# A routed feed-forward stage: table copies and gathers in another order on GpSimd, the first expert tile's transpose behind the third gathered tile, constants last

## Chip, cores and metric
One core of a Trainium2 chip. The metric is the device time of one launch in microseconds, the median of several runs. The program runs once from start to end; nothing is repeated inside it.

## What is computed
A pre-norm block on 2048 tokens of width 512, in float32: linear attention with 32 heads of 64, then a mixture of 8 experts (two chosen per token, hidden width 352). The part that matters here is the second half:

```python
scores = xf @ gate_w.T + gate_b + bias
top_scores, top_idx = jax.lax.top_k(scores, TOP_K)          # TOP_K = 2, E = 8
gates = jax.nn.softmax(top_scores, axis=-1)
comb = jnp.sum(one_hot(top_idx, E) * gates[..., None], axis=1)
h = jax.nn.silu(jnp.einsum('td,ehd->teh', xf, w1) + b1)
y = jnp.einsum('teh,edh->ted', h, w2) + b2
out = x + jnp.einsum('ted,te->td', y, comb)
```

## The kernel before, in words
Every product is made of three matmuls: each operand is split into a rounded part ("hi", on ScalarE, ACT) and the rest ("lo", on VectorE, DVE). Each engine has its own instruction list, written out by hand; semaphores join them, and an instruction behind a wait on the same engine waits too. Direct loads are issued by SyncE (SP), gathers and scatters by GpSimd (POOL).

The first 780 us are attention and the routing of each of 16 token tiles: GpSimd scatters token number and gate into a table in DRAM (`meta_dram`, line 676). What follows is the stretch around the change.

**Weights.** The expert weights go through 46 steps, k = 0 to 45: steps 0 to 21 are w1 (`W1T` is 22), steps 22 to 45 are w2, three for each expert (expert 6 is k = 40 to 42, expert 7 is k = 43 to 45). In step k TensorE transposes 128 columns' worth of the loaded weights into PSUM (`w_transpose`, line 1899, matmuls at line 1895), ACT copies the hi part (`w_hi`, line 1102, line 1105), and DVE subtracts to get the lo part (`w_lo`, line 1532, line 1536). For the steps in `PE_STEPS` TensorE subtracts instead (`subtract_hi`, line 1919) and ACT copies (line 1110). There are six PSUM banks, so step k waits for the lo part of step k - 6. The first step of an expert also waits for its load (`s_w2[e]`) and for `b2_put`, GpSimd's small copies of the bias into column 352 of the loaded weights (`put_b2`, line 722). SP loads w2 of experts 6 and 7 (`load_w2`, line 526) only once `s_metain` says that the slot table has come back (line 562).

**Slot table.** GpSimd works out which table row each slot has (lines 755 to 761), waits for all scatters (`s_meta`) and gathers the table to SBUF (`meta_in`, line 764). Then it works out the expert of each of the 39 slot tiles (`cmp`, lines 767 to 769; `padt`, `tile_expert`, lines 772 and 773). TensorE transposes the table behind step 35 (`meta_transpose`, line 1952, with `meta_put`), and DVE turns it into `slot_token` (line 1563, `ids_ready`) and `far` (line 1564); where DVE does so in its list of weight steps is the constant `META_AT`.

**Expert tiles.** A tile i is 128 slots of one expert (NS = 39 tiles). GpSimd gathers its rows (`gather`, line 694) into one of two buffers `xg`; gather(i) waits until tile i - 2 has been transposed. TensorE transposes it (`pe_gT`, line 1965, line 1970), ACT and DVE split it (`act_gT` line 1131, `dve_gT` line 1577; the lo parts carry the helper's line 1212), TensorE multiplies with w1 (`pe_h`, line 1973), ACT copies h out of PSUM (`act_h`, line 1137), TensorE transposes h (`pe_hT`, line 1982), ACT applies silu with the bias (`act_silu`, line 1143), DVE splits it (`dve_hT`, line 1581), TensorE multiplies with w2 (`pe_y`, line 1991), DVE scales by the gate (`dve_y`, line 1589), and GpSimd adds the rows to the output with an accumulating scatter (`add_out`, line 702). `hT_fill` (line 1567) writes h's constant rows (a one for the bias, zeros) once. From tile 2 on the order is a loop; tiles 0 to 2 are started by hand:

```python
            pe_gT(0, 0)                      # line 2006; w_transpose(44), w_transpose(45) behind it
            pe_gT(1, 1)                      # line 2012
            pe_h(0, first_expert)            # line 2015
            pe_h(1, expert(1))
            pe_hT(0)
            pe_gT(2, 0)
            pe_hT(1)                         # line 2020, then the loop with pe_h(2)
```

Of the kernel before, what the change touches and what calls it, by code (L numbers as in the profile page):

```python
# [30 lines left out]
ALU = mybir.AluOpType  # L31
# [16 lines left out]
E = 8  # L48
# [6 lines left out]
TW = NS + 1  # L55
# [8 lines left out]
def block_kernel(nc, x, Wq, Wk, Wv, Wo, bo, gate_w, gate_b, gbias, w1, b1, w2, b2, out):  # L64
# [110 lines left out]
    def small_sb(name, cols, dt=F32):  # L175
        at_ = used[0]
        used[0] += -(-(2 if dt is BF16 else 4) * cols // 32) * 32
        assert used[0] <= R2 + 4 * KB
        return sb(name, cols, at_, dt)

    iota_e = small_sb("iota_e", E)
    iota_j = small_sb("iota_j", TW)
# [16 lines left out]
    cmp = small_sb("cmp", TW * E)  # L199
# [26 lines left out]
    with ExitStack() as ctx:  # L226
# [3 lines left out]
        def sem(name):  # L230
            return ctx.enter_context(nc.semaphore(name))
# [96 lines left out]
        w_put = sem("w_put")  # L328
# [3 lines left out]
        w_sub_put = sem("w_sub_put")  # L332
# [40 lines left out]
        PE_STEPS = [*range(4), 11, 15, 19, 22, 25, 31, 37]  # L373
# [20 lines left out]
        wide = lambda a, n: a.unsqueeze(2).to_broadcast([P, a.shape[1], n])  # L394
        many = lambda a, n: a.unsqueeze(1).to_broadcast([P, n, a.shape[1]])
        by8 = lambda a: a.rearrange("p (n e) -> p n e", e=E)
        tiles_of, up_to, spare, past = (small[:, i * E:(i + 1) * E] for i in range(4))
# [174 lines left out]
        def _(pool):  # L572
# [121 lines left out]
            def gather(i):  # L694
                if i == 0:
                    pool.wait_ge(ids_ready, 1)
                if i >= 2:
                    pool.wait_ge(gT_put, i - 1)
                pool.indirect_dma_start(xg[:, i % 2 * D:(i % 2 + 1) * D], None, xn2_dram,
                                        bass.IndirectOffsetOnAxis(slot_token[:, i:i + 1].bitcast(U32), 0)).then_inc(s_g[i % 2], 16)  # L700
# [21 lines left out]
            def put_b2(e):  # L722
                pool.tensor_copy(w2_in[e][:, :].rearrange("p (f n) -> p f n", f=FB)[:, :, H:H + 1],
                                 b2T[:, e * FB:(e + 1) * FB].unsqueeze(2)).then_inc(b2_put, 1)
# [9 lines left out]
            def tab(ins):  # L734
                tabled[0] += 1
                ins.then_inc(table_step, 1)
                pool.wait_ge(table_step, tabled[0])

            def fold(a, n):
                while n > 1:  # L740
                    n //= 2
                    tab(pool.tensor_tensor(a[:, :, 0:n], a[:, :, 0:n], a[:, :, n:2 * n], ALU.add))
# [16 lines left out]
            fold(row8, E)  # L759
            tab(pool.tensor_tensor(row8[:, :, 0:1], row8[:, :, 0:1], iota_p[:, :].unsqueeze(1), ALU.add))  # L760
            tab(pool.tensor_scalar(meta_row[:, :].unsqueeze(1), row8[:, :, 0:1], float(MROWS - 1), None, ALU.min))
            for b in range(2):
                pool.wait_ge(s_meta[b], 16 * NT)
            pool.indirect_dma_start(meta_in[:, :], None, meta_rows, bass.IndirectOffsetOnAxis(meta_row[:, :].bitcast(U32), 0)
                                    ).then_inc(s_metain, 16)

            tab(pool.tensor_tensor(by8(cmp[:, :]), wide(iota_j[:, :], E), many(up_to, TW), ALU.subtract))
            tab(pool.tensor_scalar(by8(cmp[:, :]), by8(cmp[:, :]), 0.0, None, ALU.is_ge))
            fold(by8(cmp[:, :]), E)
            pool.wait_ge(w_put, W1T)  # L770
            pool.wait_ge(w_sub_put, W1_SUBS)
            tab(pool.tensor_copy(padt[:, :].unsqueeze(2), by8(cmp[:, :])[:, :, 0:1]))
            pool.tensor_scalar(tile_expert[:, :], padt[:, :], float(E - 1), None, ALU.min).then_inc(experts_ready, 1)
            put_b2(6)
            put_b2(7)
            gather(0)
            gather(1)
            gather(2)
            pool.wait_ge(experts_ready, 1)
            tab(pool.iota(add_iota[:, :], pattern=[[16, TW // 2], [0, 2]], base=16, channel_multiplier=0))  # L780
# [26 lines left out]
        def _(act):  # L807
# [323 lines left out]
            def act_gT(i):  # L1131
                act.wait_ge(gT_put, i + 1)
                if not (isinstance(i, int) and i < 2):
                    act.wait_ge(h_put, i)
                nc.scalar.copy(g_of(i)[0][:, :], g_bank(i)).then_inc(gT_hi_ready, 1)

            def act_h(i):
                act.wait_ge(h_put, i + 1)
                if not (isinstance(i, int) and i == 0):
                    act.wait_ge(hT_put, i)  # L1140
                nc.scalar.copy(h_in[:, :], h_bank(i)).then_inc(h_ready, 1)

            def act_silu(i, e):
                act.wait_ge(hT_put, i + 1)
                if not (isinstance(i, int) and i == 0):
                    act.wait_ge(hT_lo_ready, i)
                for b in range(HB):
                    w = min(P, H - b * P)
                    last = nc.scalar.activation(hT[0:w, b * P:(b + 1) * P], hT_bank(i)[0:w, b * P:(b + 1) * P], ACT.Silu,  # L1149
                                                bias=b1T[0:w, ds(b * E + e, 1)])  # L1150
                last.then_inc(hT_ready, 1)
# [15 lines left out]
            nc.scalar.activation(gate_e[:, :], far[:, :], ACT.Tanh, scale=0.5).then_inc(tanh_ready, 1)  # L1167
            act.wait_ge(experts_ready, 1)
            first_expert = act.value_load(tile_expert[0:1, 0:1], min_val=0, max_val=E - 1)
            act.wait_ge(hT_ones, 2)  # L1170
            act_h(0)
            act_h(1)
            act_gT(2)
            act_silu(0, first_expert)
            act_silu(1, act.value_load(tile_expert[0:1, 1:2], min_val=0, max_val=E - 1))
            with act.Fori(2, NS - 1) as i:
# [5 lines left out]
        def _(dve):  # L1182
# [28 lines left out]
            def lo(dst, src, hi):  # L1211
                return nc.vector.tensor_tensor(dst, src, f(hi), ALU.subtract)  # L1212
# [319 lines left out]
            def w_lo(k):  # L1532
                dve.wait_ge(w_hi_ready, k + 1)
                src, rows, dst = w_step(k, w1_lo, w2_lo, w_bank(k))
                hi = w_step(k, w1_hi, w2_hi, w_bank(k))[2]
                nc.vector.tensor_tensor(dst, src, f(hi), ALU.subtract).then_inc(w_lo_ready, 1)

            v = nc.vector
            META_AT = 32
            lo_steps = lambda a, b: [w_lo(k) for k in range(a, b) if k in DVE_STEPS]  # L1540

            def tiles_per_expert():
# [15 lines left out]
            lo_steps(6, 11)  # L1558
            put_slot8(NT - 1, 1)
            tiles_per_expert()  # L1560
            lo_steps(11, META_AT)
            dve.wait_ge(meta_put, 1)
            v.tensor_copy(slot_token[:, :], pX[:, 0:TW]).then_inc(ids_ready, 1)
            v.tensor_copy(far[:, :], pX[:, TW:2 * TW]).then_inc(far_ready, 1)
            lo_steps(META_AT, WSTEPS - 2)

            def hT_fill():
                dve.wait_ge(w_put, WSTEPS)
                v.memset(hT[96:128, 2 * P:3 * P], 0.0).then_inc(hT_ones, 1)
                dve.wait_ge(hT_ones, 1)  # L1570
                v.memset(hT[96:97, 2 * P:3 * P], 1.0).then_inc(hT_ones, 1)

            def put_gates():
                dve.wait_ge(tanh_ready, 1)
                v.tensor_scalar(slot_gate[:, :], gate_e[:, :], -0.5, 0.5, ALU.mult, ALU.add).then_inc(gates_ready, 1)

            def dve_gT(i):
                dve.wait_ge(gT_hi_ready, i + 1)
                lo(g_of(i)[1][:, :], g_bank(i), g_of(i)[0][:, :]).then_inc(gT_lo_ready, 1)
# [16 lines left out]
            dve_gT(0)  # L1596
            for k in range(WSTEPS - 2, WSTEPS):
                w_lo(k)
            hT_fill()
            dve_gT(1)  # L1600
            put_gates()
            dve_gT(2)
            dve_hT(0, 0)
# [21 lines left out]
        def _(pe):  # L1625
# [339 lines left out]
            def pe_gT(i, b):  # L1965
                pe.wait_ge(s_g[b], 16 * (i // 2) + 16 if isinstance(i, int) else 8 * i + (16 - 8 * b))
                if not (isinstance(i, int) and i < 2):
                    pe.wait_ge(gT_lo_ready, i)
                for n in range(FB):
                    last = nc.tensor.transpose(g_bank(i)[:, n * P:(n + 1) * P], xg[:, b * D + n * P:b * D + (n + 1) * P], ident[:, :])  # L1970
                last.then_inc(gT_put, 1)

            def pe_h(i, e):
                pe.wait_ge(gT_lo_ready, i + 1)
                if not (isinstance(i, int) and i < 2):
                    pe.wait_ge(h_ready, i)
                for n in range(FB):
                    last = three(h_bank(i), two(g_of(i), n * P, P), two((w1_hi, w1_lo), e * H + n * EH, H),
                                 n == 0, n == FB - 1)
                last.then_inc(h_put, 1)  # L1980

            def pe_hT(i):
                pe.wait_ge(h_ready, i + 1)
                if not (isinstance(i, int) and i < 2):
                    pe.wait_ge(hT_ready, i)
                for n in range(HB):
                    w = min(P, H - n * P)
                    last = nc.tensor.transpose(hT_bank(i)[0:w, n * P:(n + 1) * P], h_in[:, n * P:n * P + w], ident[:, :])  # L1988
                last.then_inc(hT_put, 1)
# [13 lines left out]
            def expert(i):  # L2003
                return pe.value_load(tile_expert[0:1, ds(i, 1)], min_val=0, max_val=E - 1)
# [9 lines left out]
            pe.wait_ge(w_act_ready, len(PE_STEPS))  # L2014
            pe_h(0, first_expert)
            pe_h(1, expert(1))
            pe_hT(0)
            pe_gT(2, 0)
            pe.wait_ge(w_lo_ready, len(DVE_STEPS))
            pe_hT(1)  # L2020
            with pe.Fori(1, NS // 2) as h:
# [35 lines left out]
```

## Time and profile before

| what | us |
|---|---|
| median of 3 runs | 1009.13 |
| lowest and highest | 1009.12, 1009.3 |
| the profiled execution's own time | 1010.6 |
| its span, first to last instruction | 1008.9 |
| TensorE busy in the span | 995.8 (99%) |
| DVE, ACT, GpSimd busy | 688.1, 513.2, 255.7 |

The granted TensorE clock is 1.0 throughout. The profiled execution took 1.5 us more than the median; its rows are from its span. Times in rows are from the span's start. A group "x8" of matmuls on one line is two weight steps or two tiles of four. The idle time in brackets is that of the engine just before the row, with what ended it; where a wait has several semaphores, the profile names the one that it takes for the last.

### The profile page before, as it was taken

What the parts mean: (1) busy time and instruction counts of PE and PEld (TensorE: products, weight loads), DVE (VectorE), ACT (ScalarE), POOL (GpSimd) and SP (SyncE); (2) the same over time, 40 slices, a digit from 0 to 9 for tenths busy, and PEclk for the clock granted to TensorE, in tenths of its full rate; (3) what the DMA queues carried; (4) which work ended last, traced back from release to release, by engine and by line L of the source; (5) the groups of instructions that cost most, each with busy time, mean ns of one, the idle gap of its engine ahead of it and who ended that gap; (6) DMA issues with size and microseconds to landing.
All of it is one profiled execution on the core that took longest, in us unless ns stands there. A gap on an engine that the chain in (4) does not pass through costs nothing.

```text
span 1008.9 us, 17463 instructions
## 1 busy us (share of the span) xinstructions
PE 995.8 (99%) x5019; PEld 839.2 (83%) x5020; DVE 688.1 (68%) x1554; ACT 513.2 (51%) x1322; POOL 255.7 (25%) x413
## 2 busy tenths in 40 slices
PE   8999999999999999999999999999999989999998
PEld 7888888888888888888788888888888879989996
DVE  6888655665666677767878778887888764544544
ACT  5444444444444447755556555555554954343442
POOL 1000000000000002222433232333333555555554
PEclk9999999999999999999999999999999999999999
DMA  7002501000000012343211121111125645555653
GB/s 263 13 30 84 209 22 40 23 21 21 21 22 21 21 63 63 105 172 116 44 44 51 42 52 42 42 42 42 42 66 149 203 123 102 107 102 101 107 108 48
DMA packets 46862, 75.35 MB, mean 75 GB/s; under 512 B 6090, under 2 KB 18555, under 8 KB 46691
## 3 DMA queue, kind: packets, MB, share of 16 engines
q1 hardware_dynamic: 37010, 56.04, 18.3%
q0 software_dynamic: 9808, 18.79, 10.2%
q8 instruction: 21, 0.34, 0.1%
q14 instruction: 23, 0.18, 0.1%
HBM read 53.14 MB, written 23.50 MB: 76 GB/s over the span
## 4 chain that ended last, share of the span: by engine, by line
PE 93%; DVE 3%; ACT 1%; DMA 1%; issue 1%; SPq 0%; POOL 0%; POOLq 0%; DVEq 0%; ACTq 0%
PE pK L1627 16%; PE pK L1629 16%; PE pK L1628 16%; PE pA L1627 6%; PE pA L1629 6%; PE pA L1628 6%; PE pX L1627 6%; PE pX L1629 5%; PE pX L1628 5%; PE pA L1761 3%; PE pT L1970 2%; PE pT L1707 2%; PE pX L1988 1%; PE pA L1895 1%; PE pK L1895 1%; DMA xn<-in_attn_hidden_states 1%
## 5 line engine op out<-in xcount | busy, mean ns | idle before, releaser
L973 ACT ACTIVATE qs<-q,nrec 128x64 f32<-128x64 f32 x512 | 129.6, 336 | 88.1 <-DVE nrec L1357 85.7
L594 POOL TENSOR_TENSOR wv_lo<-wv_in,wv_hi 128x512 fp32r<-128x512 f32 x4 | 5.2, 1296 | 403.5 <-ACT wo_hi L894 403.5
L1627 PE MATMUL pA<-k_hi,xn_hi 128*128 128x512 f32 x256 | 100.9, 394 | 0.6 <-DVE k_lo L1232 0.6
L1627 PE MATMUL pK<-wk_hi,xnT_hi 128*128 128x512 f32 (+1 forms) x256 | 100.1, 391 | 0.4 <-DVE wk_lo L1212 0.3
L1627 PE MATMUL pK<-wq_hi,xnT_hi 128*128 128x512 f32 x256 | 100.4, 392 | 0.0
L1629 PE MATMUL pK<-wq_hi,xnT_lo 128*128 128x512 f32 x256 | 99.9, 390 | 0.0
L1629 PE MATMUL pA<-k_hi,xn_lo 128*128 128x512 f32 x256 | 99.8, 390 | 0.0
L1628 PE MATMUL pK<-wk_lo,xnT_hi 128*128 128x512 f32 (+1 forms) x256 | 99.7, 390 | 0.0
L1628 PE MATMUL pA<-k_lo,xn_hi 128*128 128x512 f32 x256 | 99.7, 389 | 0.0
L1629 PE MATMUL pK<-wk_hi,xnT_lo 128*128 128x512 f32 (+1 forms) x256 | 99.7, 389 | 0.0
L1628 PE MATMUL pK<-wq_lo,xnT_hi 128*128 128x512 f32 x256 | 99.7, 389 | 0.0
L1627 PE MATMUL pX<-m_hi,qsT_hi 128*128 128x512 f32 x240 | 99.1, 413 | 0.0
L1629 PE MATMUL pX<-m_hi,qsT_lo 128*128 128x512 f32 x240 | 94.2, 393 | 0.0
L1628 PE MATMUL pX<-m_lo,qsT_hi 128*128 128x512 f32 x240 | 93.7, 390 | 0.0
L1350 DVE TENSOR_TENSOR qs<-q,ksum 128x512 f32<-128x512 f32 x64 | 51.8, 810 | 55.6 <-ACT q L967 55.6
L718 POOL DMA_INDIRECT out<-y,slot_token x38 | 66.1, 1739 | 68.8 <-DVE y L1593 43.3
L1232 DVE SCALAR_TENSOR_TENSOR k_lo<-pK,k_hi 128x512 fp32r<-128x512 f32 x64 | 44.1, 689 | 56.1 <-ACT k_hi L841 56.1
L835 ACT CAST xn_hi<-xn 128x512 fp32r<-128x512 f32 x64 | 39.8, 621 | 69.3 <-PE pA L1629 69.3
L967 ACT ACTIVATE q<-pK 128x512 f32<-128x512 f32 x64 | 38.2, 597 | 68.3 <-PE pK L1629 68.3
L841 ACT ACTIVATE k_hi<-pK 128x512 fp32r<-128x512 f32 x64 | 38.0, 595 | 66.4 <-PE pK L1629 66.3
L1149 ACT ACTIVATE hT<-pX,b1T 128x128 f32<-128x128 f32 (+1 forms) x114 | 33.2, 363 | 71.5 <-PE pX L1988 63.8
L1212 DVE TENSOR_TENSOR xn_lo<-xn,xn_hi 128x512 fp32r<-128x512 f32 x64 | 44.1, 689 | 27.6 <-ACT xn_hi L835 27.6
(291 smaller groups left out, 2446.8 us busy)
## 6 DMA issues: line engine op xcount, KB each, us to landing
w_in<-in_ffn_w SPq DMA_DIRECT2D x22, 256.0 KB, 4.2
w_in<-in_ffn_w SPq DMA_DIRECT2D x8, 704.0 KB, 5.8
xn<-in_attn_hidden_states SPq DMA_DIRECT2D x16, 256.0 KB, 6.2
wv_in<-in_attn_Wv SPq DMA_DIRECT2D x16, 256.0 KB, 2.8
wo_in<-in_attn_Wo SPq DMA_DIRECT2D x16, 256.0 KB, 3.0
wk_in<-in_attn_Wq SPq DMA_DIRECT2D x4, 1024.0 KB, 5.7
xnT_dram<-xnT SPq DMA_DIRECT2D x4, 1024.0 KB, 11.5
x_in<-in_attn_hidden_states SPq DMA_DIRECT2D x16, 256.0 KB, 2.7
```

Source lines behind the costliest of these rows:

```text
L718: pool.indirect_dma_start(out, bass.IndirectOffsetOnAxis(slot_token[:, i:i + 1].bitcast(U32), 0), rows, None, bounds_check=T - 1, oob_is_e ...
L835: nc.scalar.copy(xn_hi[:, b * D:(b + 1) * D], xn[:, ds(t * D, D)]).then_inc(xn_hi_ready, 1)
L841: nc.scalar.activation(k_hi[:, b * CW:(b + 1) * CW], pK[:, b * 512:(b + 1) * 512], ACT.Relu).then_inc(k_hi_ready, 1)
L967: nc.scalar.activation(q[:, b * CW:(b + 1) * CW], pK[:, b * 512:(b + 1) * 512], ACT.Relu).then_inc(q_ready, 1)
L973: i = nc.scalar.activation(qs[:, s], q[:, s], ACT.Copy, scale=nrec[:, b * HC + h:b * HC + h + 1])
L1149: last = nc.scalar.activation(hT[0:w, b * P:(b + 1) * P], hT_bank(i)[0:w, b * P:(b + 1) * P], ACT.Silu, bias=b1T[0:w, ds(b * E + e, 1)])
L1212: return nc.vector.tensor_tensor(dst, src, f(hi), ALU.subtract)
L1232: nc.vector.scalar_tensor_tensor(out=k_lo[:, s], in0=pK[:, b * 512:(b + 1) * 512], scalar=0.0, in1=f(k_hi[:, s]), op0=ALU.max, op1=ALU.sub ...
L1350: nc.vector.tensor_tensor(qs[:, b * CW:(b + 1) * CW], q[:, b * CW:(b + 1) * CW], ksum[:, c * CW:(c + 1) * CW], ALU.mult).then_inc(qk_ready, 1)
L1627: nc.tensor.matmul(dst, lhs[0], rhs[0], start=start, stop=False)
L1628: nc.tensor.matmul(dst, lhs[0], rhs[1], start=False, stop=False)
L1629: return nc.tensor.matmul(dst, lhs[1], rhs[0], start=False, stop=stop)
```

## The change
Four places.

1. GpSimd: the first two instructions on `cmp` move ahead of the wait for the scatters and of the table's gather.
2. GpSimd: gather(0) and gather(1) move ahead of the bias copies of experts 6 and 7.
3. DVE: weight steps 32 and 33 move ahead of the two copies out of the transposed table. Since the wait for `meta_put` no longer stands ahead of them, they get waits of their own, for step 33's transpose and for the subtraction of step 31. `hT_fill` moves behind the lo part of tile 1.
4. TensorE: the transpose of tile 2 goes ahead of that of tile 0's h. ACT: tile 2's hi part goes ahead of the copy of tile 1's h, and the wait for the constants moves down to the first silu.

```diff
@@ GpSimd
             tab(pool.tensor_scalar(meta_row[:, :].unsqueeze(1), row8[:, :, 0:1], float(MROWS - 1), None, ALU.min))
+            tab(pool.tensor_tensor(by8(cmp[:, :]), wide(iota_j[:, :], E), many(up_to, TW), ALU.subtract))
+            tab(pool.tensor_scalar(by8(cmp[:, :]), by8(cmp[:, :]), 0.0, None, ALU.is_ge))
             for b in range(2):
                 pool.wait_ge(s_meta[b], 16 * NT)
             pool.indirect_dma_start(meta_in[:, :], None, meta_rows, bass.IndirectOffsetOnAxis(meta_row[:, :].bitcast(U32), 0)
                                     ).then_inc(s_metain, 16)
 
-            tab(pool.tensor_tensor(by8(cmp[:, :]), wide(iota_j[:, :], E), many(up_to, TW), ALU.subtract))
-            tab(pool.tensor_scalar(by8(cmp[:, :]), by8(cmp[:, :]), 0.0, None, ALU.is_ge))
             fold(by8(cmp[:, :]), E)
...
             pool.tensor_scalar(tile_expert[:, :], padt[:, :], float(E - 1), None, ALU.min).then_inc(experts_ready, 1)
+            gather(0)
+            gather(1)
             put_b2(6)
             put_b2(7)
-            gather(0)
-            gather(1)
             gather(2)
@@ ACT
             first_expert = act.value_load(tile_expert[0:1, 0:1], min_val=0, max_val=E - 1)
+            act_h(0)
+            act_gT(2)
+            act_h(1)
             act.wait_ge(hT_ones, 2)
-            act_h(0)
-            act_h(1)
-            act_gT(2)
             act_silu(0, first_expert)
@@ DVE
-            META_AT = 32
+            META_AT = 34
...
-            lo_steps(11, META_AT)
+            lo_steps(11, 32)
+            dve.wait_ge(w_put, 34)
+            dve.wait_ge(w_sub_put, sum(k < 32 for k in PE_STEPS))
+            lo_steps(32, META_AT)
             dve.wait_ge(meta_put, 1)
             v.tensor_copy(slot_token[:, :], pX[:, 0:TW]).then_inc(ids_ready, 1)
...
                 w_lo(k)
+            dve_gT(1)
             hT_fill()
-            dve_gT(1)
             put_gates()
@@ TensorE
             pe_h(0, first_expert)
             pe_h(1, expert(1))
+            pe_gT(2, 0)
             pe_hT(0)
-            pe_gT(2, 0)
             pe.wait_ge(w_lo_ready, len(DVE_STEPS))
             pe_hT(1)
```

## Rows read from the trace of the kernel before

**Rows 1.** Busy time by stretch: start:end, length, engines busy (instructions), clock, DMA share, GB/s

```profile
806.80:816.03 9.23, 7.56 (x57) 6.12 (x56) 8.01 (x15) 7.44 (x15) 4.82 (x12) 1.00 0.62 213
816.03:822.89 6.86, 5.66 (x35) 4.90 (x35) 2.92 (x8) 2.82 (x8) 4.92 (x15) 1.00 0.28 80
827.68:999.20 171.52, 171.52 (x1006) 154.87 (x1004) 84.32 (x144) 67.81 (x179) 96.01 (x69) 1.00 0.56 99
```

**Rows 2.** The chain that ended last, from 811 to 816: start, length, what

```profile
811.17 1.06 PE pA L1895 x8
...
813.12 0.64 PE pK L1895 x4
...
815.09 0.70 DVE gT_lo L1212
```

**Rows 3.** Tile w_in, SP's issues from 805 to 816 (experts 6 and 7)

```profile
L527 SPq DMA_DIRECT2D w_in<-in_ffn_w x2: 367/434/501, 806.8 to 807.2; - x2
...
DMA to landing us min/median/max: 5.8/5.8/5.8
```

**Rows 4.** DMA queues from 808 to 812: packets, MB, share of 16 engines

```profile
q1 hardware_dynamic: 958, 1.33, 98.4%
```

**Rows 5.** DMA queues from 812.5 to 814

```profile
q0 software_dynamic: 136, 0.43, 76.4%
```

**Rows 6.** Timeline of GpSimd from 803 to 817: start, length, what

```profile
803.20 1.12 POOL L764 DMA_INDIRECT meta_in<-meta_dram,meta_row  x1 [2.04 <-DMA meta_dram<-vals,slot_i]
804.34 0.75 POOL L767 TENSOR_TENSOR cmp<-iota_j,small 128x320 f32<-128x320 f32 x1
805.18 1.04 POOL L768 TENSOR_SCALAR cmp<-cmp 128x320 f32<-128x320 f32 x1
...
808.83 1.06 POOL L699 DMA_INDIRECT xg<-xn_dram,slot_token  x1
810.20 0.95 POOL L699 DMA_INDIRECT xg<-xn_dram,slot_token  x1 [0.31 <-issue]
...
816.65 1.00 POOL L699 DMA_INDIRECT xg<-xn_dram,slot_token  x1 [0.50 <-POOL add_base L781]
```

**Rows 7.** Timeline of DVE from 807 to 818

```profile
807.39 0.20 DVE L1563 CAST slot_token<-pX 128x40 int32<-128x40 f32 x1 [1.75 <-PE pX L1956]
...
807.61 2.48 DVE L1536 TENSOR_TENSOR w_lo<-pA,w_hi 128x512 fp32r<-128x512 f32 x4
...
817.06 0.17 DVE L1569 MEMSET hT<- 32x128 f32 x1
...
817.50 0.69 DVE L1212 TENSOR_TENSOR g_lo<-pA,g_hi 128x512 fp32r<-128x512 f32 x1
```

**Rows 8.** Timeline of TensorE from 805 to 822

```profile
805.64 0.47 PE L1923 MATMUL pK<-w_hi,neg_ident 128*128 128x512 f32 x1
...
818.34 0.42 PE L1627 MATMUL pA<-w_hi,g_hi 128*128 x1
...
820.37 0.49 PE L1988 MATMUL pX<-ident,h_in 128*128 128x128 f32 x3
820.69 0.60 PE L1970 MATMUL pT<-ident,xg 128*128 128x128 f32 x4
821.55 0.52 PE L1988 MATMUL pA<-ident,h_in 128*128 128x128 f32 x3 [0.25 <-ACT h_in L1141]
822.89 0.42 PE L1627 MATMUL pK<-w_hi,gT_hi 128*128 x1 [0.82 <-DVE gT_lo L1212]
```

**Rows 9.** Timeline of ACT from 820 to 823

```profile
820.95 0.45 ACT L1141 COPY h_in<-pA 128x352 f32<-128x352 f32 x1 [2.19 <-PE pX L1988]
821.33 0.59 ACT L1135 CAST gT_hi<-pT 128x512 fp32r<-128x512 f32 x1
```

**Rows 10.** DMA queues from 799 to 801

```profile
q1 hardware_dynamic: 330, 0.44, 60.4%
q0 software_dynamic: 60, 0.00, 2.1%
```

## Prediction
> **What bounds the kernel now.** I read three views in turn. The busy time by stretch comes first: TensorE is busy for all of 171.52 us from 827.68 on, while it stands idle for 1.67 us of 806.80 to 816.03 and 1.20 us of 816.03 to 822.89 [rows 1]. The expert loop is full, so a change ahead of it is worth what it moves the loop's first matmul, tile 2's pe_h at 822.89 [rows 8]; that shift then rides to the end unchanged, for the closing scatters follow TensorE.
>
> The chain that ended last comes second, for the nearer limits. Ahead of tile 0's product it runs through step 43 (TensorE at 813.12, ACT, DVE), then tile 0's lo part at 815.09, ending 815.79; pe_h(0) starts at 816.03 (0.24 later) [rows 2]. Why does step 43 start only at 813.12? It is expert 7's first step. SP issued the loads of experts 6 and 7 at 806.8 and 807.2, and they land 5.8 us after issue, so at about 813.0 [rows 3]. Step 40 at 811.17 is expert 6's first step, and I read it as held by its load too: the lo part of step 34, which it also needs, is the third of the four from 807.61 on, done by about 809.5 [rows 7]. Meanwhile the 16 DMA engines are full (98.4%) and all of it is SP's queue, q1 [rows 4]; GpSimd's queue q0, with gathers issued at 808.83 and 810.20 [rows 6], moves its rows after 812.5, as q1 has run dry [rows 5].
>
> So the stretch before 816 hangs on one release: SP may load experts 6 and 7 once the slot table's gather has landed. That gather was issued at 803.20 [rows 6] and SP went on at 806.80, 3.6 us later.
>
> The timelines come third, for who is free when.
>
> **Part 1, cmp ahead of the table's gather.** Removed behind the gather: 0.75 + 1.04 us of GpSimd. Added ahead of it: the same two. GpSimd was idle for 2.04 us before 803.20, so from 801.16 [rows 6]. With the 0.09 us between these two (805.09 to 805.18) they run 801.25 to 802.00 and 802.09 to 803.13. That looks like a fit under 803.20. But the gather now follows a chained operation whose semaphore it must wait for, and gather(3), which does just that, starts 0.50 us after the operation ahead of it [rows 6]. That gives 803.63, which is **0.43 us late**. Bounds: 0 if the copies run faster or the start cost overlaps; 0.5 if they run a little slower beside DVE. I take 0.43, since the row for it is the same kind of instruction behind the same kind of wait. Behind this gather are queued: SP's two loads (+0.43, to 807.23), and TensorE's table transposes, behind which steps 36 to 39 wait. The latter is covered: TensorE then waits for expert 6's load anyway. The loads landing 0.43 later are not covered: step 43 moves to 813.55, pe_h(0) to 816.46. What GpSimd gains (the expert numbers over 1 us earlier) is worth nothing, since ids_ready holds gather(0) and TensorE reads the expert number only behind step 45.
>
> **Part 2, gathers ahead of the bias copies.** ids_ready comes at about 808.0 (the slot_token copy ended at 807.59 [rows 7] and the table lands 0.43 later), so gather(0) starts 0.14 to 0.50 us later, about 808.3 instead of 808.83, and gather(1) 1.37 us behind it, at 809.7. By [rows 4, 5] their rows move after q1 has drained whatever the issue time, so they gain nothing: cost 0. The bias copies, which ended just ahead of 808.83, now follow gather(1) and end at about 811.1; who waits is step 40, free from about 811.5 (its load). Cover 0.4 us; if the gathers' issue took longer, step 40 and then DVE's chain would slip by the excess. gather(2) still waits for tile 0's transpose, so its issue moves by the same 0.43; tile 2's transpose, now earlier, still comes about 5 us behind it.
>
> **Part 3, DVE.** DVE was free from 805.64 (1.75 us before 807.39) [rows 7]. The new waits are met at 806.11, when the subtraction of step 31 ends [rows 8]; queued behind them are steps 32 and 33 and the two copies. Steps 32 and 33 take 0.62 each (2.48 for four) [rows 7] and end near 807.5; the table, 0.43 later, lets the copies start at 807.82. Without the 0.43 the copies would be some 0.1 us late. DVE comes to step 34 over half a microsecond earlier, and step 40 doesn't gain from it while its load is last. Cost 0, gain 0. The memsets leave the front of tile 1's lo part: 817.06 to 817.50, so 0.44 us earlier, ending 817.75 instead of 818.19 [rows 7]. pe_h(1) ran from 818.34 to 820.37, 2.03 us; pe_h(0) has the same twelve matmuls from 816.03, so could hand over at 818.06. The lo part's old end, 818.19, was 0.13 past that, and the start another 0.15 behind it [rows 8]. Gain 0.13 to 0.28; I take **0.2**, the middle. The constants themselves are needed by the first silu, which ACT does behind 821.33 [rows 9], and are written at about 818.2: hidden with over 3 us.
>
> **Part 4, tile 2 ahead of h.** On TensorE the three transposes of h(0) cost 0.32 (820.37 to 820.69) [rows 8] ahead of tile 2's. On ACT the copy of h(1) stood ahead of tile 2's hi part, 0.38 from start to start [rows 9]; both ended in a tie at 821.33. With both gone tile 2's hi part starts 0.3 earlier, with the 0.2 of part 3 about 0.5 earlier, at 820.85 (in the old trace's time). DVE has nothing else then, and pe_h(2) follows the lo part as before, at 822.41. Next in line is h(1): ACT's copy comes after the hi part, at 821.35 to 821.45, and ends 0.45 later; hT(1) started 0.15 behind it (821.40, 821.55), so at 821.95 to 822.05, and with 0.33 for three transposes it is over by 822.3 to 822.4. That is nearly a tie, so I take **0.45** for the memsets' and the order's gain together. Silu of tile 0 stands behind the same two ACT instructions as before, so at the same time; its user, pe_y(0), stands behind pe_h(2), 2 us long, and doesn't come to wait.
>
> **Sum.** +0.43 - 0.45 = -0.02 us on the profiled execution: 1010.6 stays 1010.6. The median lies 1.5 us lower, 1009.13, and I carry the same difference over: 1009.1.
>
> **The rivals.** Case A, the above: +0.43 (0.3 to 0.5) and -0.45 (-0.5 to -0.3), so 1009.0 to 1009.3.
>
> Case B: the table's gather isn't late. If the 0.50 us start cost was already inside the 2.04 us idle (scatters landed at 802.7 and the gather took its time), or the two copies are quicker in an idle stretch, then 803.2 stays. For it: the idle is put down to a DMA, whose landing isn't shown. Then only -0.45 is left: 1008.7, with the bounds 1008.5 to 1008.8.
>
> Case C, slower: gathers 0 and 1 are issued half a microsecond sooner and SP's loads 0.43 later, so gather rows get in before expert 7's weights. The engines moved 1.33 MB from 808 to 812 with the first packets only after 808.3 [rows 4], so nearly 0.4 MB/us; a gather of 128 rows of 2 KB is 0.26 MB, so one ahead costs 0.66 us, both 1.33. Against: no packet of q0 from 808 to 812 although gather(0) had been issued by 809.9 [rows 4, 6]. For: earlier, small scatters of q0 do have 60 packets beside 330 of q1 within 2 us [rows 10]. It decides once gather(0)'s descriptors stand ready before SP's last ones. Net 0.43 + 0.66 - 0.45 = +0.6, or +1.3 with both: 1009.8 to 1010.4. The Trainium skill (DMA: Bandwidth & Descriptors, section Queues, rings and completion order) says that each DMA engine takes turns between the queues that have work, packet by packet; by that rule the two queues would share, and earlier gathers would push the loads back, up to this case. The rows show no sharing where gather(0) waited, so I give it a low chance.
>
> Case D: part 4's gain is lost in the near tie (hT(1) late, since it now waits for an ACT copy that comes 0.4 later), or the bias copies pass 811.5. Then +0.43 - 0.45 + 0.2 to 0.4: 1009.3 to 1009.5.
>
> **How the numbers follow.** A 0.45, B 0.25, C 0.15, D 0.15. The likeliest is A, so 1009.1. For 8 in 10 the range takes all of A, D and B, and the lower half of C: 1008.4 to 1010.0, with 0.1 to spare below B's lowest. What a measurement of this kernel can tell from no change is about 0.2%, here 2.0 us. No case reaches that: B is -0.6 at most and C +1.3. I leave 0.02 for faster and 0.03 for slower by something that I don't see; same 0.95.
>
> **What would show it.** In the changed profile: cmp's two instructions end near 803.1, and the table's gather starts at 803.6 (A) or 803.2 (B). SP's loads start 3.6 us behind it. Step 43 at 813.5 (A), 813.1 (B), or over 814 (C); in C there would be q0 packets between 809 and 812. From pe_h(0) to pe_h(2) 6.86 us become about 6.4; if hT(1) ends last there, it is D. Wrong would be: a loop that is no longer full, or pe_h(2) more than 0.7 us off 822.9.

## The result, and the profile after

The changed kernel takes 1011.69 us (median of 14 runs, 1010.01 to 1012.88) against 1009.4 (14 runs, 1008.7 to 1010.78): +2.3 us, a ratio of 1.002 with a 95% interval of 1.0013 to 1.0027. Forecast were 1009.1 and a range up to 1010.0. The changed kernel is **slower**, by an amount that is small (0.2%; by a bound of 2% the two are the same) but clear of its interval, and that no case of the prediction reached. Three executions of the kernel before among those beside the later kernels took 1422 to 4806 us; they are left out of every ratio and count.

The profiled execution shows almost none of that. It took 1010.63 us with a span of 1008.9, the kernel before 1010.6 and 1008.9. Both are single executions; before's lies near the upper end of its 14 runs, after's near the lower end. So two traces side by side look the same, and the medians don't. Below, h(1) is tile 1's h as ACT copies it out of PSUM, and hT(1) is its transpose on TensorE (`pe_hT`). The busy time by stretch, after, in the stretches of [rows 1]:

```profile
806.80:816.03 9.23, 7.45 (x58) 6.34 (x57) 7.67 (x15) 7.42 (x15) 3.76 (x7) 1.00 0.62 213
816.03:822.89 6.86, 5.21 (x35) 4.72 (x34) 3.06 (x9) 2.69 (x8) 4.98 (x14) 1.00 0.27 78
827.68:999.20 171.52, 171.52 (x1006) 154.88 (x1004) 84.37 (x143) 67.81 (x179) 95.99 (x69) 1.00 0.56 99
```

The loop is as full as before. TensorE is idle for 1.65 us of the second stretch, where it was 1.20. Its timeline there, after (what answers to [rows 8]):

```profile
810.95 1.06 PE L1898 MATMUL pA<-ident,w_in 128*128 128x128 f32 x8 [0.97 <-DMA w_in<-in_ffn_w]
...
812.91 0.63 PE L1898 MATMUL pK<-ident,w_in 128*128 128x128 f32 x4 [0.46 <-issue]
...
815.83 0.43 PE L1630 MATMUL pK<-w_hi,gT_hi 128*128 x1 [0.34 <-DVE gT_lo L1212]
...
817.85 0.32 PE L1630 MATMUL pA<-w_hi,g_hi 128*128 x1
...
819.77 0.60 PE L1973 MATMUL pT<-ident,xg 128*128 128x128 f32 x4
820.21 0.49 PE L1991 MATMUL pX<-ident,h_in 128*128 128x128 f32 x3
821.68 0.52 PE L1991 MATMUL pA<-ident,h_in 128*128 128x128 f32 x3 [0.98 <-ACT h_in L1141]
822.87 0.42 PE L1630 MATMUL pK<-w_hi,gT_hi 128*128 x1 [0.67 <-issue]
```

pe_h(1) at 817.85 follows pe_h(0) at once, as planned, and is 0.49 ahead of its old time. But pe_h(0) itself, at 815.83, is 0.20 ahead of its old time, where the forecast had it 0.43 behind. The table's gather is only 0.12 late in this trace (GpSimd's timeline, after):

```profile
802.00 1.03 POOL L763 TENSOR_SCALAR cmp<-cmp 128x320 f32<-128x320 f32 x1
803.32 1.12 POOL L766 DMA_INDIRECT meta_in<-meta_dram,meta_row  x1 [0.29 <-POOL cmp L763]
```

SP went on 3.43 us behind it instead of 3.60, and step 43 came 6.16 us behind SP's issue instead of 6.32. Then hT(1) waits 0.98 us for the copy of h(1), and pe_h(2) a further 0.67 for "issue", that is for nothing that another engine does. Tile 2's lo part had long been there, by DVE's timeline (with ACT's two rows ahead of it):

```profile
820.41 0.59 ACT L1135 CAST gT_hi<-pT 128x512 fp32r<-128x512 f32 x1 [1.91 <-PE pT L1973]
821.09 0.45 ACT L1141 COPY h_in<-pA 128x352 f32<-128x352 f32 x1
```

```profile
821.03 0.69 DVE L1212 TENSOR_TENSOR gT_lo<-pT,gT_hi 128x512 fp32r<-128x512 f32 x1 [2.94 <-ACT gT_hi L1135]
```

It ended at 821.72, and pe_h(2) started 1.15 us later. What stands between hT(1) and pe_h(2) is the fetch of tile 2's expert number by TensorE's own sequencer, at the head of the loop. The view of that line's instructions, after:

```profile
L2007 PEldq TENSOR_LOAD <-tile_expert x2: 311/312/312, 816.7 to 821.9; - x2
L2007 PEldq FUSED_REGOPS  x2: 151/154/156, 817.1 to 822.3; - x2
L2007 PEldq SEQ_ASSERT  x2: 18/18/18, 817.3 to 822.5; - x2
```

The load starts at 821.9, behind hT(1), and what belongs to it ends past 822.5. The kernel before fetched at 821.9 too, which its view shows in the same way, with DVE's row for the lo part behind it:

```profile
L2004 PEldq TENSOR_LOAD <-tile_expert x1: 311/311/311, 821.9 to 821.9; - x1
```

```profile
821.95 0.69 DVE L1212 TENSOR_TENSOR gT_lo<-pT,gT_hi 128x512 fp32r<-128x512 f32 x1 [3.66 <-ACT gT_hi L1135]
```

So in the kernel before the lo part (over at 822.64) and the fetch (over past 822.5) met at nearly the same time, and the profile named only the first of them [rows 8].

### The profile page after: what moved, and what is told of

It is laid out like the page before. It is cut to its first block, busy times and chain, and to the rows that moved or that the text cites. A ratio compares the mean times of both kernels' runs of the same rounds, so it can differ in the third digit from the quotient of the medians.

```text
span 1008.9 us, 17464 instructions
## 1 busy us (share of the span) xinstructions
PE 995.6 (99%) x5019; PEld 839.2 (83%) x5020; DVE 690.0 (68%) x1554; ACT 513.3 (51%) x1322; POOL 255.2 (25%) x413
## 4 chain that ended last, share of the span: by engine, by line
PE 93%; DVE 3%; DMA 2%; ACT 1%; issue 1%; POOL 0%; SPq 0%; POOLq 0%; DVEq 0%; ACTq 0%
PE pK L1630 16%; PE pK L1632 16%; PE pK L1631 16%; PE pA L1630 6%; PE pA L1632 6%; PE pA L1631 6%; PE pX L1630 5%; PE pX L1632 5%; PE pX L1631 5%; PE pA L1764 3%; PE pT L1973 2%; PE pT L1710 2%; PE pX L1991 1%; PE pA L1898 1%; PE pK L1898 1%
## 5 line engine op out<-in xcount | busy, mean ns | idle before, releaser
L1350 DVE TENSOR_TENSOR qs<-q,ksum 128x512 f32<-128x512 f32 x64 | 55.1, 861 | 53.9 <-ACT q L967 53.9
```

The lines of the kernel that those rows point to most:

```text
L1350: nc.vector.tensor_tensor(qs[:, b * CW:(b + 1) * CW], q[:, b * CW:(b + 1) * CW], ksum[:, c * CW:(c + 1) * CW], ALU.mult).then_inc(qk_ready, 1)
```

## The experiments

The theories differ in where the 2.3 us lie: in part 4 (S), in GpSimd's parts (G), or nowhere in particular (L). The four first kernels split the change.

**e1_order4: part 4 alone.**

```diff
-            act.wait_ge(hT_ones, 2)
             act_h(0)
-            act_h(1)
             act_gT(2)
+            act_h(1)
+            act.wait_ge(hT_ones, 2)
...
-            pe_hT(0)
             pe_gT(2, 0)
+            pe_hT(0)
```

> The kernel before with part 4 alone: TensorE transposes tile 2 ahead of tile 0's h, ACT does tile 2's hi part ahead of h(1), and waits for the constants at the first silu. Theory S (the loss is local: the new order gathers TensorE's idle time into fewer, longer pieces and something downstream then runs slower): this run alone shows the whole loss, +2.3 us on 1009.4, and the rest of the change none. Theory G (the loss comes from GpSimd's and the DMA queues' new order): 0 here, within 0.5 us. Theory L (the loss has no place in the changed stretch; it comes with any changed program, through how the instructions lie in memory or how the start falls): every variant is off by an amount of its own, between 0 and +3 us, and they do not add up. In the trace pe_h(2) starts at 822.9 as before, because the expert number for it is only fetched by TensorE's sequencer behind hT(1).

Measured: 1010.29 us, ratio 1.0011 (1.0002 to 1.002) to 1009.35. TensorE's timeline of this kernel:

```profile
814.94 0.42 PE L1627 MATMUL pK<-w_hi,gT_hi 128*128 x1 [0.34 <-DVE gT_lo L1212]
...
821.20 0.52 PE L1988 MATMUL pA<-ident,h_in 128*128 128x128 f32 x3 [0.98 <-ACT h_in L1141]
822.55 0.42 PE L1627 MATMUL pK<-w_hi,gT_hi 128*128 x1 [0.83 <-issue]
```

pe_h(0) to pe_h(2) takes 7.61 us instead of 6.86: part 4 is a loss of 0.75 us by itself. The eleven runs fall into two groups: eight at 1009.5 to 1010.6, three at 1011.4 to 1012.1, and these three have a mean granted clock of 0.997, the others 0.998 to 1.0.

**e2_no_order4: parts 1 to 3.** The changed kernel with the diff above undone, except that the wait for the constants stays at the silu.

> The changed kernel with part 4 undone (TensorE's and ACT's old order, the constants' wait just ahead of the first silu). Theory S: back to 1009.4 within 0.5. Theory G: 1011.7, the whole loss stays. Theory L: off by an amount of its own. In the trace pe_h(1) starts at once behind pe_h(0), hT(1) is no later than before, so pe_h(2) should be 0.2 to 0.5 us earlier than 822.9 if only the lo part and the sequencer's fetch hold it.

Measured: 1009.75 us, 1.0001 (0.9992 to 1.001); all runs at clock 0.998 or more. pe_h(0) to pe_h(2) is 6.38 us. So Theory S holds for most of the loss if part 4 is taken out of the change (1.9 us of the 2.3 go with it), but e1 with part 4 alone showed only 0.9. And step 43 came 7.04 us behind SP's issue, where it was 6.32. The DMA queues of this kernel from 812 to 812.5 show what goes with it:

```profile
q0 software_dynamic: 61, 0.19, 102.2%
q1 hardware_dynamic: 3, 0.00, 1.8%
```

Three last packets of SP's load (q1) go out in the midst of the gathers' rows (q0), 5.9 us or more behind SP's issue, and expert 7's load isn't complete before them.

**e3_gpsimd12: parts 1 and 2; e4_dve3: part 3.** Each is the kernel before with these lines of the diff alone; e4 (and h2 and i2 below) have ACT's wait for the constants at the first silu as well.

> The kernel before with parts 1 and 2 alone (cmp ahead of the table's gather, gathers 0 and 1 ahead of the bias copies). Theory G: the whole loss, +2.3 us. Theory S: 0 within 0.5. Theory L: an amount of its own. In the trace the table's gather starts at 803.3, as in the changed kernel.

> The kernel before with part 3 alone (weight steps 32 and 33 ahead of the table copies, constants behind tile 1's lo part; ACT's wait for them at the first silu). Theories S and G: 0 within 0.5, or 0.1 to 0.3 faster as pe_h(1) follows pe_h(0) at once. Theory L: an amount of its own.

Measured: e3 1010.04 us, 1.0006 (0.9997 to 1.0015); e4 1008.73, 0.9993 (0.9984 to 1.0002). The parts' shifts from 1009.35 are +0.9, +0.7 and -0.6; they add up to +1.0, and the change has +2.3. Each shift is uncertain by about 0.9 us, and e3's and e4's intervals reach no difference, so they count only together with the traces. Each shift has a matching piece there, which speaks against Theory L in its strong form, but 1.3 us are missing.

**f1_after_again: the changed kernel, unaltered.**

> The changed kernel once more, unaltered, for a second trace, since its 14 runs lie between 1010.0 and 1012.9 and the first trace (1010.63) is among the fastest. Eight of the 14 have a mean granted clock of 0.997. TensorE idles only at the end, for 4.9 us, which by the records explains down to 0.998. Theory K (clock): in those runs the clock is granted at its lower level for one stretch in the middle too, right behind the idle pieces between 820.7 and 822.9, and costs about 1.6 us there. Then a trace with 0.997 has such a stretch between 821 and 830, and its loop is late by 1.6 us. Theory T (tail): the extra time lies behind the last product, at the closing scatters, and the stretch up to there is as in the first trace.

(Counted again, seven of the fourteen have 0.997, not eight.) Measured: 1012.67 us, clock 0.997, and the trace has it. Busy time by stretch; the column ahead of the last two is the granted clock:

```profile
822.00:824.00 2.00, 1.13 (x5) 0.91 (x6) 1.16 (x3) 0.83 (x4) 1.10 (x1) 0.89 0.01 4
824.00:826.00 2.00, 2.00 (x8) 2.00 (x8) 0.92 (x2) 0.87 (x3) 0.00 (x0) 0.50 0.47 139
826.00:828.00 2.00, 2.00 (x11) 1.85 (x11) 0.00 (x0) 0.84 (x2) 0.16 (x1) 0.76 0.00 0
828.00:830.00 2.00, 2.00 (x13) 1.63 (x12) 1.00 (x2) 0.18 (x1) 0.78 (x1) 1.00 0.23 43
```

The clock stands at its lower level, 1.2 GHz instead of 2.4, through 824 to 826 and parts of the stretches on either side. Ahead of it TensorE had been idle for 0.98 and 0.67 us. What it costs is in the timeline of that run:

```profile
822.21 0.52 PE L1991 MATMUL pA<-ident,h_in 128*128 128x128 f32 x3 [0.98 <-ACT h_in L1141]
823.39 0.53 PE L1630 MATMUL pK<-w_hi,gT_hi 128*128 x1 [0.67 <-issue]
...
826.95 0.62 PE L1973 MATMUL pT<-ident,xg 128*128 128x128 f32 x4
```

The twelve matmuls of pe_h(2) take 3.56 us from 823.39 to 826.95, against 2.02 in the first trace: 1.54 us, and pe_h(2) to the last matmul grows by the same, from 180.74 to 182.27. Theory K holds; Theory T falls, since nothing is lost at the tail.

**f2_fill: the idle piece filled.**

```diff
             pe.wait_ge(w_lo_ready, len(DVE_STEPS))
+            keep_clock(8)
             pe_hT(1)
```

> The changed kernel with 8 idle transposes of the identity on TensorE between hT(0) and hT(1), into a PSUM bank that hT(1) overwrites. They lie in the 0.98 us in which TensorE waits for h(1), and should not delay hT(1) (8 x 0.11 us). Theory K: no run with clock 0.997 any more; median 1010.3 or a little below, 1.4 under the changed kernel's 1011.7. Theory T: 1011.7 as before, with half of the runs slow.

Measured: 1010.49 us, 1.001 (1.0001 to 1.0019) to 1009.5. hT(1) isn't held, and no run of eleven is at 0.997 (one is at 1012.1 with clock 1.0, so something else; what, isn't known). TensorE's timeline of this kernel, with the eight transposes (L1669):

```profile
820.71 1.04 PE L1669 MATMUL pA<-ident 128*128 128x128 f32 x8
821.76 0.55 PE L1991 MATMUL pA<-ident,h_in 128*128 128x128 f32 x3
822.94 0.42 PE L1630 MATMUL pK<-w_hi,gT_hi 128*128 x1 [0.62 <-issue]
```

The second idle piece, 0.62 us, is still there. Eight useless transposes take 1.2 us off the changed kernel.

**f3_idle: the kernel before with a later copy of h(1).**

```diff
             act_h(0)
+            act.wait_ge(h_put, 2)
+            act.wait_ge(hT_put, 1)
+            for n in range(6):
+                nc.scalar.activation(nrm[:, n:n + 1], eps[:, :], ACT.Silu)
             act_h(1)
```

> The kernel before with six one-column activations on ACT between the wait for hT(0) and the copy of h(1): the copy, hT(1), the fetch of the expert number and pe_h(2) all move back by the time that they take, 0.6 to 1.2 us, and TensorE is idle for that much more in one piece. Theory K: the delay itself, plus a share of runs that are slower by a further 1.6 us at clock 0.997, so a median of 1010.5 to 1012. Theory T: 1009.4 plus the delay and nothing else, no second group of runs.

Measured: 1010.76 us, 1.001 (1.0001 to 1.0019). The activations take 0.9 us, pe_h(2) is 7.50 behind pe_h(0). Six runs of twelve are at 0.997, with a median of 1011.6; the others' is 1010.1. This is the changed kernel's picture (idle pieces of 1.03 and 0.70 us around hT(1)), from the kernel before and one delay. Its profiled run is one of the six:

```profile
822.00:824.00 2.00, 1.76 (x7) 1.77 (x8) 1.01 (x3) 0.83 (x4) 0.04 (x1) 0.66 0.42 131
824.00:826.00 2.00, 2.00 (x9) 1.93 (x8) 0.92 (x2) 0.35 (x2) 0.00 (x0) 0.50 0.03 8
826.00:828.00 2.00, 2.00 (x12) 1.68 (x11) 0.69 (x1) 0.87 (x2) 0.94 (x1) 0.98 0.00 0
```

**f4_part1, g3_part1_late, g4_part2: GpSimd's parts apart.** f4 is the kernel before with part 1, g4 with part 2, and g3 is f4 and:

```diff
             put_b2(7)
+            pool.wait_ge(w_put, 39)
             gather(0)
```

> The kernel before with part 1 alone (cmp ahead of the table's gather). The four traces with and without it have the gather starting 6.0 us (with) and 5.2 to 5.8 us (without) behind the last scatter's issue. If that is the whole of the GpSimd parts' cost: +0.4 us, 1009.8, the same as parts 1 and 2 together. If the order of the gathers costs too (their rows ahead of expert 7's load, seen once in the second experiment's trace): +0.4 here against +0.7 for both.

> The kernel before with part 1, and a wait ahead of gather(0) for the transpose of step 38, so that the gather is issued some 2 us behind SP's loads as before and not 1.1 us. Theory Q (part 1 costs twice: the table's gather is 0.45 us late, and the early gather's rows get in ahead of the last packets of expert 7's weights, up to 0.7 us more): step 43 comes 6.2 to 6.3 us behind SP's issue, not 6.4 to 7.0, and the median is 1009.9, against 1010.4 for part 1 alone. If the second cost has nothing to do with when the gather is issued: 1010.4.

> The kernel before with part 2 alone: gathers 0 and 1 ahead of the bias copies. gather(0) is then issued 0.3 to 0.4 us earlier, some 1.6 us behind SP's loads. Theory Q: between nothing and +0.2 us, 1009.4 to 1009.6, as the gather still comes late. If the order of gathers and copies itself costs (step 40 waiting for the copies): step 40 starts later than 4.4 us behind SP's issue.

Measured: f4 1010.39 us, 1.0004 (0.9996 to 1.0013) to 1009.5; g3 1010.26, 1.0009 (1.0 to 1.0018) to 1009.43; g4 1009.68, 0.9999 (0.999 to 1.0008). By these medians part 1 carries the GpSimd parts' cost, though f4's interval reaches no difference. In g3 step 43 comes 6.32 us behind SP's issue, in f4 6.41: the late wait brings back only 0.1, in the trace as in the median. So as far as this tells the cost of part 1 alone is the table's later gather, and Theory Q's second half is worth little without parts 2 and 3. Step 40 in g4 starts 4.45 us behind SP's issue (before 4.37): the bias copies don't hold it.

**g1_hoist, g2_best, h3_best2, i1_best3: the fetch moved.** The fetch of tile 2's expert stands further ahead, and the loop's first pass is written out. g1 has this on the changed kernel, the others on parts 3 and 4 with GpSimd's order as before. In g1 and g2 it stands with tile 1's ahead of pe_h(1), in h3 both stand ahead of pe_h(0), in i1:

```diff
             pe_hT(0)
+            expert_2 = expert(2)
             pe.wait_ge(w_lo_ready, len(DVE_STEPS))
             pe_hT(1)
-            with pe.Fori(1, NS // 2) as h:
+            for i in (2, 3):
+                pe_h(i, expert_2 if i == 2 else expert(3))
+                pe_gT(i + 1, 1 - i % 2)
+                pe_y(i - 2, i % 2, expert(i - 2))
+                pe_hT(i)
+            with pe.Fori(2, NS // 2) as h:
```

> The changed kernel with the number of tile 2's expert fetched ahead of pe_h(1) instead of behind hT(1), and the loop's first pass (tiles 2 and 3) written out so that it can be used. Theory F (tile 2's product is held by the sequencer's fetch, 1.2 to 1.35 us behind hT(1), and not by its lo part): pe_h(2) follows hT(1) at once, 6.1 to 6.3 us behind pe_h(0) instead of 7.04, and the long idle piece is shorter, so hardly a run at clock 0.997; median 1009.4 to 1009.7. If instead the lo part of tile 2 holds it: 7.0 us and 1011.7 stay.

> Parts 3 and 4 with the fetch moved as in g1, but GpSimd's order as before. Theory F with the costs measured so far (GpSimd's parts +0.7, part 3 -0.4, part 4 with the fetch moved -0.3 instead of +0.7): 1008.5 to 1008.8, below the kernel before (1009.4) and no slower than part 3 alone (1008.7). Without Theory F: 1009.7.

> Parts 3 and 4, GpSimd's order as before, and the expert numbers of tiles 1 and 2 both fetched ahead of pe_h(0), where TensorE waits anyway (in g2 they stood between pe_h(0) and pe_h(1) and held the latter by 0.3 us). pe_h(1) 2.02 us and pe_h(2) 6.2 to 6.3 us behind pe_h(0); median 1008.5, 0.9 under the kernel before and 0.2 under part 3 alone; no run at clock 0.997. If the two fetches hold pe_h(0) instead: 0.3 later, 1008.8.

> Parts 3 and 4, GpSimd's order as before, and the number of tile 2's expert fetched between hT(0) and hT(1), in the 0.98 us in which TensorE waits for h(1). Step 43 to pe_h(2) was 9.77 us in the kernel before, 9.39 with part 3 alone, 9.52 and 9.47 with the fetch further ahead (g2, h3), where it held pe_h(1) or pe_h(0). If the fetch fits into the wait: 9.1, pe_h(2) 6.2 us behind pe_h(0), median 1008.4 to 1008.7. If it holds hT(1): 9.3 to 9.5 and 1008.8 to 1009.1.

Measured: g1 1010.0 us, 1.0006 (0.9997 to 1.0015); g2 1009.26, 0.9998 (0.9989 to 1.0007); h3 1009.11, 0.9997 (0.9988 to 1.0007), all to 1009.4; i1 1008.77, 0.9992 (0.9983 to 1.0001) to 1009.61. No run of the 44 is at 0.997. In g1 and g2 the two fetches held pe_h(1) by 0.3 us, in h3 they held pe_h(0) by 0.4, so these came short of what was expected. In i1 the fetch fits into the wait. TensorE's timeline of i1:

```profile
818.97 0.49 PE L1991 MATMUL pX<-ident,h_in 128*128 128x128 f32 x3
820.44 0.52 PE L1991 MATMUL pA<-ident,h_in 128*128 128x128 f32 x3 [0.98 <-ACT h_in L1141]
820.72 0.40 PE L1630 MATMUL pK<-w_hi,gT_hi 128*128 x1
```

pe_h(2) comes 0.28 us behind hT(1) instead of 1.19, with the same 0.98 us of waiting ahead of hT(1), and 0.24 behind the end of its lo part. In the 15 traces whose fetch wasn't moved, pe_h(2) stands 1.18 to 1.35 us behind hT(1), also where the lo part had ended 1.3 us before (e1, h1). Theory F holds: what stood behind hT(1) was the hold, and not the lo part. One thing isn't split: with the first pass written out the loop's entry moves away from pe_h(2) too. Of the 0.9 us won, the rows put 0.6 on the fetch (821.9 to past 822.5); the rest may be the loop's entry. And with an idle piece of 0.98 us but nothing behind hT(1), the clock fell in none of these 44 runs. i1 has the largest lead of all kernels here, 0.8 us under the kernel before; its median is 2.9 under that of the changed one. Against the kernel before its interval just reaches no difference, and e4 with part 3 alone has 0.6, so which of the two is the better stays open.

**h1_parts34, h2_parts13, i2_dve3_again.**

> The changed kernel without the GpSimd parts: parts 3 and 4 alone. Traces so far price part 3 at -0.4 us and part 4 at +0.7 (pe_h(0) to pe_h(2): 6.86 before, 6.4 with part 3, 7.6 with part 4, 7.04 with both), so undisturbed runs at 1009.6. Theory K1 (the clock falls only for the idle pieces around hT(1), whatever comes before): a third to a half of the runs at clock 0.997 and 1011.2, as in the kernel with part 4 alone (3 of 11) and the changed one (8 of 15). Theory K2 (the longer idle around step 43, that the GpSimd parts bring, takes a share in it): fewer than a fifth here.

> The kernel before with parts 1 and 3. In four of five traces with parts 1, 2 and 3 together step 43 comes 6.8 to 7.0 us behind SP's issue, in the traces without part 3 or without part 1 6.2 to 6.4. If the last weight packets fall behind the gather's rows whenever parts 1 and 3 are there: about 7.0 here. If it takes part 2 as well: 6.2 to 6.4. Median: 1009.4 +0.6 (gather) -0.4 (part 3) = 1009.6, or 1010.2 with late weights.

> Part 3 alone, as in e4, which came out 0.6 us under the kernel before with an interval that reached it. If the 0.4 us that its trace shows is real: 0.4 to 0.7 us under the kernel before again. If e4 was luck: within 0.2 us of it.

Measured: h1 1009.99 us, 1.0006 (0.9997 to 1.0015), with three runs of eleven at 0.997, the same share as part 4 alone. The lower clock needs no GpSimd part. The share lies between what K1 (a third to a half) and K2 (under a fifth) expected; whether the GpSimd parts raise it (8 of 15 in the changed kernel) is more than these counts can tell. h2 1009.77, 1.0003 (0.9994 to 1.0012), step 43 at 6.25 us: with parts 1 and 3 the last weight packets were not late. i2 1009.39, 0.9997 (0.9987 to 1.0006) to 1009.61: part 3 is 0.2 us ahead here and 0.6 in e4, both times on the side of its trace's 0.4, but not beyond its interval in either. By what was expected of i2, e4's 0.6 was luck in part.

The distances from the traces on which all this rests, in us:

| kernel | last scatter issue to table gather | SP's issue to step 43 | pe_h(0) to pe_h(1) | pe_h(0) to pe_h(2) | runs at clock 0.997 |
|---|---|---|---|---|---|
| before | 5.83 | 6.32 | 2.31 | 6.86 | 1 of 120 |
| changed, two traces | 5.99, 6.00 | 6.16, 7.00 | 2.02, 2.02 | 7.04, 7.03 | 8 of 15 |
| e1, part 4 | 5.25 | 6.23 | 2.31 | 7.61 | 3 of 11 |
| e2, parts 1 to 3 | 5.99 | 7.04 | 2.03 | 6.38 | 0 of 11 |
| e3, parts 1 and 2 | 6.06 | 6.31 | 2.31 | 6.86 | 0 of 11 |
| e4, part 3 | 5.56 | 6.27 | 2.02 | 6.47 | 0 of 11 |
| f3, delay | 5.42 | 6.21 | 2.30 | 7.50 | 6 of 12 |
| h1, parts 3 and 4 | 5.69 | 6.24 | 2.01 | 7.19 | 3 of 11 |
| i1, fetch moved | 4.91 | 6.15 | 2.01 | 6.12 | 0 of 11 |

(The 120 runs of the kernel before are those that stood beside e, f, g and h.)

## Why the prediction was wrong, point by point

**Part 4 had the wrong sign.** Forecast was a gain of about 0.3 us; alone it costs 0.75. The step that failed is "pe_h(2) follows the lo part as before, at 822.41", with "Next in line is h(1) ... nearly a tie". Two chains lead into pe_h(2): one through tile 2's lo part, which the profile named, and one through the copy of h(1), hT(1) and the fetch of the expert number. In the kernel before they ended nearly together; part 4 shortened the first and lengthened the second. From the start of tile 2's transpose to pe_h(2) the prediction had 2.24 us (820.17, which is 0.2 ahead of the old 820.37, to 822.41); measured are 3.10 (819.77 to 822.87). Nearly all of the 0.86 between them is the fetch and the loop's entry: pe_h(2) was put at most 0.1 us behind the end of hT(1), so at most 0.46 behind its start, and it stands 1.19 behind it. That wait was not in the sum at all. The rest is the copy of h(1), put 0.5 to 0.6 us behind the start of the hi part and measured at 0.68 (820.41, 821.09). The rows could have told: pe_h(2) stood 1.34 us behind hT(1) [rows 8], and the loads' view was one question away. Case D had the right place, a near tie that is lost, but priced it at 0.2 to 0.4 us and had no fetch in it.

That pe_h(2) still came at 822.87, within the prediction's own bound of 0.7 us around 822.9, is chance: this trace was 0.20 ahead at pe_h(0) and lost 0.18 behind it.

**The lower clock was in no case.** I had the clock down as 1.0 throughout and took idle time on TensorE at its face value. By the runs it has a second price: with the idle pieces of 0.98 and 0.67 us around hT(1) or a little longer ones, three to eight runs in eleven to fifteen drop to 1.2 GHz for a stretch that costs 1.54 us. This is why the median moved by 2.3 us, while the runs of the changed kernel that are not at 0.997 have a median of 1010.6, only 1.2 above the kernel before (two of these seven are at 1011.6 and 1011.7; why, isn't known). f2 and f3 show it from both sides: with the idle piece filled the lower clock is gone, with like pieces made in the kernel before it comes. What these runs show is both pieces together: the second alone (f2) or the first alone (g1, g2, h3, i1) brought it in none of 55 runs. The Trainium skill (TensorE: Matmul & The Clock Gate, Part 1: The HAM clock gate) says that a block of the chip watches how busy TensorE has been and passes only half of the clock's pulses when it was idle. The rows of f1 agree, with 0.50 for 824 to 826. I had left the page out, since the trace of the kernel before showed the full clock in the loop.

**Part 1 was right in kind, with one trace too little behind it.** The gather follows a chained operation, starts 0.3 us behind it (forecast 0.5), and is then at 5.99 to 6.06 us behind the last scatter's issue in all nine traces that have part 1. In ten traces without it the gather starts at 4.91 to 5.83, 5.34 in the mean. So the loss is 0.67 us on average, against 0.43 forecast. The start cost was put 0.2 too high, and the profiled execution of the kernel before happened to have the latest landing of them all, 0.5 behind the mean, so that its own trace shows only 0.16. The medians of e3 and f4, 0.7 and 0.9 us up, fit this, though neither is beyond its interval.

**Part 2 and Case C.** Part 2 alone shows no cost (g4). But in four of five traces with parts 1, 2 and 3 together step 43 comes 6.8 to 7.0 us behind SP's issue, and the last two to six weight packets lie among the gathers' rows. That is Case C at its small end, 0.6 us and not 1.3. Late packets and late step go together in these traces; no run moves the one without the other. What makes it happen in some executions and not in others stays open; e3, f4 and h2 don't have it.

The reading that q0 moves only when q1 has run dry left out half a microsecond. Between the stretches of [rows 4] and [rows 5], from 812 to 812.5, the kernel before had both:

```profile
q1 hardware_dynamic: 89, 0.10, 61.1%
q0 software_dynamic: 24, 0.10, 52.2%
```

So the end of a load was shared there too. Ahead of it the hold is real: gather(2), issued at 814.65 with both queues quiet, had its first packets between 816 and 816.5, 1.4 to 1.9 us later, while gather(0), issued at 808.83, had none before 812. The rule of the Trainium skill that was weighed (DMA: Bandwidth & Descriptors, Queues, rings and completion order) fits the end of the load better than my reading did, and the stretch up to 812, in which q1 alone went, worse.

**Part 3 was right by the traces**: forecast 0.2 us, measured 0.29 to pe_h(1)'s start and 0.4 to pe_h(2). It is the one part whose traces gain; in the medians of e4 and i2 the gain isn't beyond the interval.

**The sum.** By the traces +0.67 (part 1), -0.4 (part 3), +0.66 (part 4 on top of part 3: 6.38 to 7.04) are +0.9; the late packets add 0.6 in four of five traces; together that roughly meets the 1.2 us of the runs without the lower clock. The lower clock adds 1.5 in half of them. The prediction's own bounds have two slips without effect: Case A's lower end should be 1008.9 and Case B's 1008.6, by its -0.5.

## What to carry to other kernels

Before moving work ahead of a wait, list every chain into the instruction that counts, the engine's own register loads included: a profile names the last releaser, and a second chain that is only just hidden takes over unseen. Idle time on TensorE isn't only its own length: here two pieces of 0.98 and 0.67 us close together cost the clock too in half of the runs, and one of 0.98 alone didn't, so compare the spread and the clocks of several runs, not two single traces. And where work waits on a transfer, read the transfer's landing from more than one execution before filling its wait to the brim.

## What was not expected of the hardware

- After idle pieces of 0.98 and 0.67 us, the granted clock was at its lower level in some executions and not in others of the same program: 8 of 15 for the changed kernel, 1 of 120 for the one before, whose pieces were 0.25 and 0.82 us. With 0.98 us alone it was 0 of 44.
- On ACT the copy of h(1) started 0.09 us behind the end of tile 2's hi part (0.68 us from start to start), while in the old order the hi part started 0.07 ahead of that copy's end (0.38). Both have semaphore waits of their own, and why only one overlaps isn't shown by any run.
- A fetch of one number by TensorE's sequencer took 0.31 us by its row, 0.6 with the two small instructions behind it, and 1.18 to 1.35 us passed from the start of the three transposes ahead of it to the matmul behind it (the loop's entry lies there too); hidden in a wait it cost nothing.
- A gather's first packets came 1.4 to 1.9 us behind its start on quiet queues, and over 3.1 us behind it while SP's queue was full.
